# Spreading a head's projections between its tiles, sharing the mask's pieces among three engines, and all transfers of p on one queue, in a graph attention kernel with layer norm

## Chip, cores and metric

One Trainium2 chip, one core. The metric is the device time of the kernel in microseconds (us), the median of several executions; a profile is one execution. PE (TensorE) multiplies, DVE (VectorE), ACT (ScalarE) and POOL (GpSimd) work on elements, SP (SyncE) only issues transfers (DMAs); ACT can issue them too.

## What is computed

```python
def reference(x, adj, Wq, Wk, Wv, Wout):          # x (2048, 256), adj (2048, 2048), W (256, 2048)
    q = (x @ Wq).reshape(8, 2048, 256)            # a head is 256 rows of x @ W, read as 2048 x 256
    k = (x @ Wk).reshape(8, 2048, 256)
    v = (x @ Wv).reshape(8, 2048, 256)
    a = q @ k.T / 16 + adj + adj                  # per head
    a = where(adj == 0, -1e6, a); a = softmax(a); a = where(adj == 0, 0, a)
    out = (a @ v).transpose(1, 0, 2).reshape(2048, 2048) @ Wout
    return layernorm(x + out)                     # over the last axis, eps 1e-5
```

Nearly all of adj is zero (about 1 element in 256 is not).

## The kernel before

Every factor of a product is split into a high part and a low part (`k_split`, `q_split`, `v_split`, `p_split`, `w_slot`), the high by an ACT copy, the low by a subtraction on DVE or POOL, and a product is the sum of three partial products. There are 8 heads, and in each 16 tiles of 128 query rows (`tau` counts tiles over all heads, 0 to 127; h is the head and t the tile in it).

A tile goes through these steps. PE makes the scores of 128 rows against 2048 columns in four banks (`scores`, L367). DVE adds the mask M (adj, and minus a huge number where adj is zero) and takes maxima (`score`, L591), then the row's maximum (L603). ACT takes exp over the whole row (`exp_tile`, L497). DVE transposes p in blocks of 32 (`turn`, L611), DMAs move the blocks to their places in `p_turned` (`shuffle`: for each quarter i of the row four transfers j, two issued by SP at L257 and two by ACT at L516). ACT writes the high part of each quarter (`hi_p`, L506), POOL the low part (`lo_p`, L449). PE multiplies by v three tiles later (`values(tau - LAG)`, L386 to L390), with Wout already in v, and DVE divides by the row's sum and adds to y (`add_y`, L633, L636).

A head needs 33 projections: k0 to k7, q0 to q7, vt0 to vt7 (x times Wv, transposed), v0 to v7 (vt times Wout) and the transpose of its rows of x. Each takes a bank, a copy on ACT (L491) and a subtraction on DVE (L579, L575). The k and q0 come in one row ahead of tile 0, the vt and v in one row ahead of tile 3, and q1 to q7 within the even tiles. The weights come through five slots (loaded at L226, high part L483, low part L438). Scores and projections take the six banks in turn, in the order in which `in_order` names them.

In head 0 the mask is built too, one tile ahead. `build(t, q)` takes a piece of adj (128x512, loaded at L242 into one of two places in the unused part of `y_acc`), marks its zeros (L645) and writes the mask's piece (L650), both on DVE. `store_m` saves each tile's mask in memory, and ACT loads it again for heads 1 to 7. At the end 15 tiles are normalised (L696) after the last y is complete, then the last one.

Each engine runs its list in order. Waits on semaphores alone tie the lists together, and an engine or a queue that waits holds all that stands behind it.

## Time and profile before

| | |
|---|---|
| median of 3 runs | 2012.87 us (2012.28 to 2017.43) |
| the profiled execution's own time | 2015.95 us |
| its span, first to last instruction | 2014.2 us |
| busy: PE, DVE, ACT, POOL | 92%, 57%, 41%, 45% of the span |
| PE busy in the first fifth and later | 4 to 8 tenths, then 9 or more |
| mean granted clock of PE | 0.96 of 2.4 GHz |
| transfers of p | 2048 of 64 KB, half each on SP and ACT, 2.0 and 2.1 us from issue to landing |

A busy share says how long an engine had an instruction in work, not that it set the pace. A wait row says which engine stood idle, and what came last before it went on. Times within the span count from its first instruction.

### The profile page before, as it was taken

Reading aid. Unit: us, or ns where it says so; the run is one execution under the profiler, and the core shown is the slowest. Engines: PE = TensorE matmul, PEld = TensorE weight load, DVE = VectorE, ACT = ScalarE, POOL = GpSimd, SP = SyncE. Lnnn points to the kernel's source line nnn. Section 1 sums busy time; section 2 is a strip of 40 time slices with the busy share of each in tenths; the row PEclk is TensorE's granted clock in tenths of the full one; section 3 lists DMA queues with packets and bytes.
Section 4 is the critical chain, followed back from the end, with each engine's and each line's share of the span. In section 5 each row is a group of like instructions: output and inputs, shape, how many; then the busy total and the mean of one; then the engine's idle time right before and its main releaser. Section 6 shows DMA issues by size and latency. Waiting matters only on the chain.

```text
span 2014.2 us, 29280 instructions
## 1 busy us (share of the span) xinstructions
PE 1854.8 (92%) x10272; PEld 1611.9 (80%) x10272; DVE 1152.2 (57%) x2356; ACT 819.3 (41%) x1364; POOL 904.8 (45%) x718
## 2 busy tenths in 40 slices
PE   6487768799999999999999999899999999999996
PEld 5376657698888888898887988798888988888885
DVE  6567877455555555545564555555554555655664
ACT  3232212443454443444444533453444443544432
POOL 4133222545454454544445454554454454544442
PEclk9698888899999999999999999999999999999998
DMA  5645555646665566556665466555665466654663
GB/s 171 186 129 175 170 177 184 182 135 190 193 192 167 149 181 193 173 150 178 197 202 148 149 186 191 173 158 166 189 194 165 145 184 189 202 165 136 182 177 95
DMA packets 186931, 345.97 MB, mean 172 GB/s; under 512 B 39328, under 2 KB 96672, under 8 KB 170400
## 3 DMA queue, kind: packets, MB, share of 16 engines
q10 hardware_dynamic: 65280, 184.62, 29.8%
q1 hardware_dynamic: 121504, 159.47, 28.5%
q8 instruction: 82, 1.34, 0.3%
q14 instruction: 65, 0.53, 0.1%
HBM read 190.84 MB, written 18.87 MB: 104 GB/s over the span
## 4 chain that ended last, share of the span: by engine, by line
PE 75%; POOL 2%; issue 2%; DMA 2%; DVE 1%; ACT 1%; SPq 0%; ACTq 0%; POOLq 0%; DVEq 0%
PE bank L367 31%; PE y_bank L390 19%; PE bank L339 13%; PE y_bank L388 10%; PE y_bank L386 1%; POOL w_slot L438 1%; DMA raw_w<-in_L_gnn_Wk_dram 1%; POOL p_split L449 1%; DVE y_acc L696 0%; DVE vt_split L579 0%; DMA m_dram<-m_sb 0%; SPq L257 0%; ACT t_p L497 0%; ACT w_slot L483 0%; DMA y_acc<-in_adj_dram 0%
## 5 line engine op out<-in xcount | busy, mean ns | idle before, releaser
L449 POOL TENSOR_TENSOR p_split<-p_turned,p_split 128x512 fp32r<-128x512 f32 x512 | 649.2, 1297 | 844.2 <-ACT p_split L506 843.0
L367 PE MATMUL bank<-k_split,q_split 128*128 128x512 f32 x3072 | 800.0, 396 | 27.5 <-issue 16.7
L390 PE MATMUL y_bank<-v_split,p_split 128*128 128x512 f32 x1920 | 710.6, 403 | 0.0
L367 PEld LDWEIGHTS bank<-k_split,q_split 128*128 128x128 f32 x3072 | 584.9, 191 | 142.4 <-issue 18.2
L497 ACT ACTIVATE t_p<-t_p,small 128x2048 f32<-128x2048 f32 x128 | 257.1, 2009 | 871.8 <-DVE small L603 866.6
L591 DVE CUSTOM_DVE_ANT_0 t_p<-bank,m_sb 128x512 f32<-128x512 f32 x512 | 351.0, 687 | 427.2 <-PE bank L367 408.4
L388 PE MATMUL y_bank<-v_split,p_split 128*128 128x256 f32 x2048 | 561.3, 285 | 0.0
L390 PEld LDWEIGHTS y_bank<-v_split,p_split 128*128 128x128 f32 x1920 | 367.3, 191 | 79.6
L388 PEld LDWEIGHTS y_bank<-v_split,p_split 128*128 128x128 f32 x2048 | 395.3, 193 | 23.3
L438 POOL TENSOR_TENSOR w_slot<-raw_w,w_slot 128x512 fp32r<-128x512 f32 x192 | 249.2, 1306 | 243.9 <-ACT w_slot L483 240.9
L339 PE MATMUL bank<-x_t,w_slot 128*128 128x256 f32 x2304 | 312.0, 290 | 39.1 <-POOL w_slot L438 28.3
L339 PEld LDWEIGHTS bank<-x_t,w_slot 128*128 128x128 f32 x2304 | 301.1, 198 | 49.6 <-POOL w_slot L438 29.8
L611 DVE STREAM_TRANSPOSE blocks<-t_p 128x2048 f32<-128x2048 f32 x128 | 295.6, 2309 | 75.0 <-ACT t_p L497 70.0
L506 ACT ACTIVATE p_split<-p_turned 128x512 fp32r<-128x512 f32 x512 | 283.5, 617 | 10.5 <-issue 5.6
L483 ACT ACTIVATE w_slot<-raw_w 128x512 fp32r<-128x512 f32 x192 | 118.4, 624 | 65.4 <-DMA raw_w<-in_L_gnn_Wv_dram 26.0
L339 PE MATMUL bank<-w_out,vt_split 128*128 128x256 f32 x768 | 105.5, 288 | 23.2 <-DVE vt_split L579 23.2
L339 PEld LDWEIGHTS bank<-w_out,vt_split 128*128 128x128 f32 x768 | 97.8, 194 | 26.6 <-DVE vt_split L579 26.6
L633 DVE SCALAR_TENSOR_TENSOR y_acc<-y_bank,small,y_acc 128x256 f32<-128x256 f32 x128 | 61.9, 484 | 63.6 <-PE y_bank L390 63.2
L386 PE MATMUL y_bank<-v_split,p_split 128*128 128x512 f32 x128 | 54.7, 428 | 44.4 <-POOL p_split L449 44.4
L645 DVE TENSOR_SCALAR_CACHE_REDUCE zero_mark<-y_acc 128x512 uint8<-128x512 f32 x64 | 43.8, 684 | 68.0 <-DMA y_acc<-in_adj_dram 67.7
L579 DVE TENSOR_TENSOR k_split<-bank,k_split 128x512 fp32r<-128x512 f32 x64 | 43.5, 686 | 64.0 <-ACT k_split L491 64.0
L650 DVE SCALAR_TENSOR_TENSOR m_sb<-zero_mark,y_acc 128x512 f32<-128x512 uint8 x64 | 77.5, 1211 | 3.3
(43 smaller groups left out, 630.1 us busy)
## 6 DMA issues: line engine op xcount, KB each, us to landing
m_sb<-m_dram ACTq DMA_DIRECT2D x112, 1024.0 KB, 4.9
p_turned<-blocks SPq DMA_DIRECT2D x1024, 64.0 KB, 2.0
p_turned<-blocks ACTq DMA_DIRECT2D x1024, 64.0 KB, 2.1
raw_w<-in_L_gnn_Wk_dram SPq DMA_DIRECT2D x64, 256.0 KB, 3.8
y_acc<-in_adj_dram SPq DMA_DIRECT2D x64, 256.0 KB, 3.2
raw_w<-in_L_gnn_Wq_dram SPq DMA_DIRECT2D x64, 256.0 KB, 3.2
m_dram<-m_sb SPq DMA_DIRECT2D x16, 1024.0 KB, 3.9
raw_w<-in_L_gnn_Wv_dram SPq DMA_DIRECT2D x64, 256.0 KB, 3.4
```

The lines of the kernel that those rows point to most:

```text
L339: mm = nc.tensor.matmul(dst[:, o * R:(o + 1) * R], left[:, a, k, o * P:(o + 1) * P], right[:, b, k, :], start=(i == 0), stop=(i == len(TER ...
L367: mm = nc.tensor.matmul(dst[:], q[:, a, k, f * P:(f + 1) * P], k_split[:, kk, k, b * BANK:(b + 1) * BANK], start=(i == 0), stop=(i == len( ...
L388: nc.tensor.matmul(y[:, 0:D], lo, v_split[:, j, HI], start=False, stop=False)
L390: mm = nc.tensor.matmul(y[:], hi, v_split[:, j].rearrange("p s d -> p (s d)"), start=False, stop=last)
L438: nc.gpsimd.tensor_tensor(w[:, LO], raw_slot[n % SLOTS][:], w[:, HI].bitcast(F32), ALU.subtract).then_inc(w_lo, 1)
L449: nc.gpsimd.tensor_tensor(lo, p_turned[:, i * BANK:(i + 1) * BANK].rearrange("p (j b) -> p j b", b=QUAD), hi.bitcast(F32), ALU.subtract).t ...
L483: nc.scalar.activation(w[:, HI], raw_slot[n % SLOTS][:], ACT.Copy).then_inc(w_hi, 1)
L497: nc.scalar.activation(t_p[:], t_p[:], ACT.Exp, bias=neg_max[:, t:t + 1], scale=1.0, accum_out=row_sum[:, t:t + 1]).then_inc(exp_done, 1)
L506: nc.scalar.activation(by_chunk(p_split[tau % 2][:, HI])[:, :, i, :], p_turned[:, i * BANK:(i + 1) * BANK].rearrange("p (j b) -> p j b", b ...
L591: nc.vector.tensor_tensor_reduce(out=t_p[:, b * BANK:(b + 1) * BANK], in0=bank[r][:], in1=m_sb[tau % 2][:, b * BANK:(b + 1) * BANK], scale ...
L611: nc.vector.transpose(blocks[tau % 2][:].rearrange("p (q j b) -> p j q b", q=QUADS, b=QUAD), t_p[:].rearrange("p (j q b) -> p j q b", q=QU ...
L650: nc.vector.scalar_tensor_tensor(out=m_sb[t % 2][:].rearrange("p (c r) -> p c r", c=C)[:, :, q * rows:(q + 1) * rows], in0=zero_mark[:].re ...
```

## The change

1. **Projections between the tiles.** `due(tau, b)` lists what stands behind bank b of tile tau, on every engine. In head 0 only k0, k1 and q0 come before tile 0; k2 to k7 stand between its banks, vt and v in tiles 0 to 2. In later heads k0 to k6 stand in tile 15 of the head before, k7 in tile 0, vt and v in tiles 1 to 3.
2. **The mask.** Of the four pieces of a tile the odd ones are built as before. The even ones are marked by DVE, scaled by ACT (`scale_mark`) into the mask, and adj is added by POOL (`add_adj`).
3. **Adjacency a tile ahead.** The loads for tile t + 2 stand behind the transfers of tile t − 1. There are four places up to piece 43, the last of tile 10, and two from then on.
4. **Transfers.** All 16 of a tile are issued by SP, none by ACT.
5. **Norm in parts.** Tiles 0 to 11 are normalised after y of tile 12 (iteration 128), 12 to 14 after y of tile 14, and the last at the end.

```diff
-        Y_LATE = TILES - 4
-        adj_chunk = [y_acc[:, Y_LATE + 2 * i:Y_LATE + 2 * i + 2, :].rearrange("p a d -> p (a d)") for i in range(2)]
-        zero_mark = sbuf("zero_mark", [P, BANK], U8)
+        Y_MID, Y_LATE = TILES - 8, TILES - 4
+        adj_place = [y_acc[:, Y_MID + 2 * i:Y_MID + 2 * i + 2, :].rearrange("p a d -> p (a d)") for i in range(4)]
+        FOUR_PLACES = 11 * BANKS
+        adj_at, adj_nth, adj_uses = [], [], [0] * 4
+        for a in range(TILES * BANKS):
+            place = a % 4 if a < FOUR_PLACES else 2 + a % 2
+            adj_uses[place] += 1
+            adj_at.append(place)
+            adj_nth.append(adj_uses[place])
...
+        FIRST_V = {(0, 3): (("vt", 0), ("vt", 1)), (1, 0): (("v", 0), ("vt", 2)), (1, 1): (("v", 1), ("vt", 3)),
...
+        NEXT_K = {(TILES - 1, 0): (0,), (TILES - 1, 1): (1, 2), (TILES - 1, 2): (3, 4), (TILES - 1, 3): (5, 6)}
+        def due(tau, b):
+            h, t = divmod(tau, TILES)
+            if h >= H:
+                return
+            for c in FIRST_K.get((t, b), ()) if h == 0 else ((C - 1,) if (t, b) == (0, 0) else ()):
+                yield "k", h, c
+            if t % 2 == 0 and t <= LAST_Q and b == (3 if tau == 0 else 1):
+                yield "q", h, t // 2 + 1
+            for kind, c in (LATER_V if h else FIRST_V).get((t, b), ()):
+                yield kind, h, c
+            if h + 1 < H:
+                if (t, b) == (TURN_X, 1):
+                    yield "x", h + 1
+                if (t, b) == (TILES - 2, 2):
+                    yield "q", h + 1, 0
+                for c in NEXT_K.get((t, b), ()):
+                    yield "k", h + 1, c
...
-            if t == 0:
-                for c in range(C):
-                    in_order(("k", h, c))
-                in_order(("q", h, 0))
-            if t == VALUES_FROM:
-                for c in range(C + 1):
-                    if c < C:
-                        in_order(("vt", h, c))
-                    if c:
-                        in_order(("v", h, c - 1))
             for b in range(BANKS):
                 in_order(("s", tau, b))
-                if b == 1 and t % 2 == 0 and t <= LAST_Q:
-                    in_order(("q", h, t // 2 + 1))
-                if b == 1 and t == TURN_X and h + 1 < H:
-                    in_order(("x", h + 1))
+                for key in due(tau, b):
+                    in_order(key)
...
+        EARLY_NORM = TILES - 4
+        NORM_PARTS = [slice(0, EARLY_NORM), slice(EARLY_NORM, TILES - 1), slice(TILES - 1, TILES)]
...
+        def m_piece(a):
+            t, q = divmod(a, BANKS)
+            rows = BANK // C
+            return m_sb[t % 2][:].rearrange("p (c r) -> p c r", c=C)[:, :, q * rows:(q + 1) * rows]
...
                     t, q = divmod(a, BANKS)
-                    if a >= 2:
-                        sp.wait_ge(m_chunk, a - 1)
-                    sp.dma_start(adj_chunk[a % 2], adj_rows[t // 2, t % 2][:, q * BANK:(q + 1) * BANK]
-                                 ).then_inc(adj_loaded[a % 2], 16)
+                    place = adj_at[a]
+                    if adj_nth[a] > 1:
+                        m_of(max(b for b in range(a) if adj_at[b] == place))
+                    sp.dma_start(adj_place[place], adj_rows[t // 2, t % 2][:, q * BANK:(q + 1) * BANK]
+                                 ).then_inc(adj_loaded[place], 16)
...
-                    for j in range(QUADS // 2):
+                    for j in range(QUADS):
...
+                load_w(SLOTS + len(START))
                 for tau in range(ALL + 1):
                     h, t = divmod(tau, TILES)
                     if h == 0:
+                        if t == 0:
+                            for i in range(BANKS):
+                                load_adj(BANKS + i)
+                            load_wout(0)
                         store_m(t)
-                        if t == 1:
-                            for f in range(HALVES):
-                                sp.dma_start(y_tokens[:, f, :Y_LATE // 2], x_tokens[f][:, :Y_LATE // 2]
-                                             ).then_inc(y_init, 16)
+                        if t == 2:
+                            load_y(0, Y_MID // 2, y_init)
+                        if t == 10:
+                            load_y(Y_MID // 2, Y_LATE // 2, y_mid)
...
+                        if tau < ALL:
+                            load_w(w_by[tau, i] + SLOTS)
                         if tau:
                             shuffle(tau - 1, i)
-                        if h == 0 and t + 1 < TILES:
-                            load_adj((t + 1) * BANKS + i)
-                    if opens:
-                        load_w_behind("q", h, 0)
-                    if sums:
-                        load_w_behind("vt", h, C - 1)
-                    if tau < ALL and t % 2 == 0 and t <= LAST_Q:
-                        load_w_behind("q", h, t // 2 + 1)
+                        if h == 0:
+                            load_adj((t + 2) * BANKS + i)
...
                 def project_x(key):
+                    wait_emptied(("x", key[1]))
                     pe.wait_ge(w_lo, w_order[key] + 1)
                     project(key, w_of(key), x_t)
+                def project_v(key):
+                    kind, h, c = key
+                    pe.wait_ge(wout_lo, h + 1)
+                    wait_emptied(("vt", h, c))
+                    project(key, vt_split[c % 2], w_out)
...
+                        for key in due(tau, g):
+                            if key[0] == "x":
+                                turn_x(key[1])
+                            elif key[0] == "v":
+                                project_v(key)
+                            else:
+                                project_x(key)
...
+                def add_adj(a):
+                    t, q = divmod(a, BANKS)
+                    m = m_piece(a)
+                    pool.wait_ge(m_scaled, a // 2 + 1)
+                    nc.gpsimd.tensor_tensor(m, m, adj_place[adj_at[a]].rearrange("p (r c) -> p c r", c=C),
+                                            ALU.add).then_inc(m_by_pool, 1)
...
+                    for b in range(BANKS):
+                        if 2 <= tau < ALL + 2:
+                            lo_p(tau - 2, b)
+                        if tau + 1 < TILES and b in (1, 3):
+                            add_adj((t + 1) * BANKS + b - 1)
+                        for key in due(tau, b):
+                            if key in w_order:
+                                lo_w(w_order[key] + 3)
...
-                def shuffle(tau, i):
-                    if i == 0:
-                        act.wait_ge(turned, tau + 1)
-                    if tau:
-                        act.wait_ge(p_lo, 4 * (tau - 1) + i + 1)
-                    for j in range(QUADS // 2, QUADS):
-                        act.dma_start(p_turned[quad(j), i * BANK:(i + 1) * BANK],
-                                      blocks[tau % 2][quad(i), j * BANK:(j + 1) * BANK]).then_inc(shuffled[i], 16)
...
+                def scale_mark(a):
+                    t, q = divmod(a, BANKS)
+                    if t >= 2:
+                        act.wait_ge(m_stored, 16 * (t - 1))
+                        act.wait_ge(max_ready, t - 1)
+                    act.wait_ge(marked, a + 1)
+                    nc.scalar.activation(m_piece(a), zero_mark[0][:].rearrange("p (r c) -> p c r", c=C), ACT.Copy,
+                                         scale=-BIG).then_inc(m_scaled, 1)
...
+                    dve.wait_ge(adj_loaded[adj_at[a]], 16 * adj_nth[a])
+                    if q % 2 == 0 and a:
+                        dve.wait_ge(m_scaled, a // 2)
+                    if q % 2 and a > 1:
+                        dve.wait_ge(m_by_dve, a // 2)
+                    nc.vector.tensor_scalar(mark[:], adj_piece, 0.0, None, ALU.is_equal, ALU.add,
                                             accum_out=chunk_count[:, q:q + 1]).then_inc(marked, 1)
-                    if q == 0 and t >= 2:
-                        dve.wait_ge(m_stored, 16 * (t - 1))
-                    dve.wait_ge(marked, a + 1)
-                    nc.vector.scalar_tensor_tensor(
-                        out=m_sb[t % 2][:].rearrange("p (c r) -> p c r", c=C)[:, :, q * rows:(q + 1) * rows],
-                        in0=zero_mark[:].rearrange("p (r c) -> p c r", c=C), scalar=-BIG,
-                        in1=adj_chunk[a % 2].rearrange("p (r c) -> p c r", c=C),
-                        op0=ALU.mult, op1=ALU.add).then_inc(m_chunk, 1)
+                    if q % 2:
+                        if t >= 2:
+                            dve.wait_ge(m_stored, 16 * (t - 1))
+                        dve.wait_ge(marked, a + 1)
+                        nc.vector.scalar_tensor_tensor(
+                            out=m_piece(a), in0=mark[:].rearrange("p (r c) -> p c r", c=C), scalar=-BIG,
+                            in1=adj_piece.rearrange("p (r c) -> p c r", c=C),
+                            op0=ALU.mult, op1=ALU.add).then_inc(m_by_dve, 1)
...
+                            if tau + 1 < TILES:
                                 build(t + 1, b)
+                        for key in due(tau, b):
+                            lo_of(key)
                     if tau == ALL:
                         denominator(tau - 1)
-                all_vars(0, slice(0, TILES - 1))
-                all_vars(1, slice(TILES - 1, TILES))
-                inverse_std(0, slice(0, TILES - 1))
-                normalise(0, TILES - 1)
-                inverse_std(1, slice(TILES - 1, TILES))
-                normalise(TILES - 1, TILES)
+                        all_vars(0, NORM_PARTS[0])
+                        inverse_std(0, NORM_PARTS[0])
+                        normalise(NORM_PARTS[0])
+                    if tau == ALL + LAG - 1:
+                        all_vars(1, NORM_PARTS[1])
+                        inverse_std(1, NORM_PARTS[1])
+                        normalise(NORM_PARTS[1])
+                all_vars(2, NORM_PARTS[2])
+                inverse_std(2, NORM_PARTS[2])
+                normalise(NORM_PARTS[2])```

On DVE, in a tile of head 0 from the turn on, before: `score` is the row of two ISA instructions, and each L645 (mark) is followed by its L650 (mask piece); `m_chunk` counts pieces.

```order
L611 STREAM_TRANSPOSE blocks<-t_p 128x16x4x32 [waits shuffled3,shuffled2,exp_done,shuffled1,shuffled0]
L591 ISA t_p,small<-bank,m_sb 128x512 [waits m_chunk,turned,scores_done]
L591 ISA small 128x1
L618 SCALAR_TENSOR_TENSOR small<-small 128x1 [waits floor_done]
L622 RECIPROCAL small<-small 128x1 [waits denom_ready]
L645 TENSOR_SCALAR zero_mark,small<-y_acc 128x512 [waits m_chunk,adj_loaded0]
L650 SCALAR_TENSOR_TENSOR m_sb<-zero_mark,y_acc 128x8x64 [waits marked,m_stored]
L591 ISA t_p,small<-bank,m_sb 128x512 [waits m_chunk,scores_done]
```

The same place after the change.

```order
L626 STREAM_TRANSPOSE blocks<-t_p 128x16x4x32 [waits shuffled3,shuffled2,exp_done,shuffled1,shuffled0]
L606 ISA t_p,small<-bank,m_sb 128x512 [waits m_by_pool,m_by_dve,turned,scores_done]
L606 ISA small 128x1
L633 SCALAR_TENSOR_TENSOR small<-small 128x1 [waits floor_done]
L637 RECIPROCAL small<-small 128x1 [waits denom_ready]
L664 TENSOR_SCALAR zero_mark,small<-y_acc 128x512 [waits m_scaled,adj_loaded0]
L606 ISA t_p,small<-bank,m_sb 128x512 [waits scores_done]
L606 ISA small 128x1
L664 TENSOR_SCALAR zero_mark,small<-y_acc 128x512 [waits m_by_dve,adj_loaded1]
L670 SCALAR_TENSOR_TENSOR m_sb<-zero_mark,y_acc 128x8x64 [waits marked,m_stored]
```

Piece 0 has lost its mask instruction on DVE, piece 1 keeps it, and the tile's first score now waits for the mask of POOL (`m_by_pool`).

On SP, at the start of a tile of head 0, before: the store of the mask, two transfers of p for a quarter, then the load of a piece of adj.

```order
L249 DMA m_dram<-m_sb 128x2048 [waits m_stored,m_chunk]
L257 DMA p_turned<-blocks 32x512 [waits p_lo,turned]
L257 DMA p_turned<-blocks 32x512
L242 DMA y_acc<-in_adj_dram 128x512 [waits m_chunk]
L257 DMA p_turned<-blocks 32x512 [waits p_lo]
```

The same place after the change.

```order
L289 DMA m_dram<-m_sb 128x2048 [waits m_stored,m_by_dve,m_by_pool]
L302 DMA p_turned<-blocks 32x512 [waits p_lo,turned]
L302 DMA p_turned<-blocks 32x512 x3
L281 DMA y_acc<-in_adj_dram 128x512 [waits m_by_pool]
L302 DMA p_turned<-blocks 32x512 [waits p_lo]
```

Four transfers stand where two stood, and the load between the quarters waits for a mask piece of the next tile, half of the time one of POOL's.

On PE, between the last banks of head 0 and the row of k of head 1, before (L339 is a projection, L388 and L390 are values).

```order
L388 MATMUL y_bank<-v_split,p_split 128x256
L390 MATMUL y_bank<-v_split,p_split 128x512
L339 MATMUL bank<-x_t,w_slot 128x256 [waits emptied2,w_lo,emptied3]
L339 MATMUL bank<-x_t,w_slot 128x256 x11
L339 MATMUL bank<-x_t,w_slot 128x256 [waits emptied3,w_lo]
L339 MATMUL bank<-x_t,w_slot 128x256 x11
L339 MATMUL bank<-x_t,w_slot 128x256 [waits emptied4,w_lo]
```

The same after the change, in tile 15 of head 0.

```order
L401 MATMUL bank<-k_split,q_split 128x512 [waits emptied1]
L401 MATMUL bank<-k_split,q_split 128x512 x5
L366 MATMUL bank<-x_t,w_slot 128x256 [waits emptied2,w_lo,emptied3]
L366 MATMUL bank<-x_t,w_slot 128x256 x11
L366 MATMUL bank<-x_t,w_slot 128x256 [waits emptied3,w_lo]
L366 MATMUL bank<-x_t,w_slot 128x256 x11
L422 MATMUL y_bank<-v_split,p_split 128x256
L424 MATMUL y_bank<-v_split,p_split 128x512
```

Nine projections in a row have become one or two between scores and values; elsewhere `due` sets up to five (behind bank 1 of tile 2).

## Rows read from the trace of the kernel before

**Rows 1.** Busy time by stretch, of windows in us.

```profile
core 0: us, PE busy (x) PEld busy (x) DVE busy (x) ACT busy (x) POOL busy (x), PEclk, DMA share, GB/s
150.00:345.00 195.00, 146.27 (x669) 120.82 (x669) 148.50 (x308) 50.54 (x82) 54.61 (x44) 0.86 0.55 172
410.00:1980.00 1570.00, 1542.15 (x8703) 1345.47 (x8702) 868.26 (x1776) 688.00 (x1144) 753.98 (x595) 0.99 0.60 174
```

**Rows 2.** The turns in five stretches: count, ns min/median/max, first and last start.

```profile
L611 DVE STREAM_TRANSPOSE blocks<-t_p x4: 2300/2302/2311, 46.7 to 135.5; 128x2048 f32<-128x2048 f32 x4
...
L611 DVE STREAM_TRANSPOSE blocks<-t_p x12: 2300/2302/2311, 135.5 to 344.5; 128x2048 f32<-128x2048 f32 x12
...
L611 DVE STREAM_TRANSPOSE blocks<-t_p x3: 2300/2302/2312, 344.5 to 389.4; 128x2048 f32<-128x2048 f32 x3
...
L611 DVE STREAM_TRANSPOSE blocks<-t_p x97: 2300/2311/2315, 389.4 to 1780.8; 128x2048 f32<-128x2048 f32 x97
...
L611 DVE STREAM_TRANSPOSE blocks<-t_p x16: 2303/2311/2314, 1780.8 to 1980.2; 128x2048 f32<-128x2048 f32 x16
```

**Rows 3.** Waits from 150 to 345 us: total, times, longest in us.

```profile
PE y_bank L386 <- POOL p_split L449: 42.0, 9, 6.2
DVE zero_mark L645 <- DMA y_acc<-in_adj_dram: 38.7, 15, 4.2
```

**Rows 4.** Timeline of one tile of head 0: start, us, engine, idle before.

```profile
270.63 1.15 SPq L257 DMA_DIRECT2D p_turned<-blocks  x2
...
271.83 0.58 SPq L242 DMA_DIRECT2D y_acc<-in_adj_dram  x1
...
275.49 0.69 DVE L645 TENSOR_SCALAR_CACHE_REDUCE zero_mark<-y_acc 128x512 uint8<-128x512 f32 x1 [3.51 <-DMA y_acc<-in_adj_dram]
```

**Rows 5.** Issues of p's transfers on SP, and the page's time to landing.

```profile
499.62 3.12 SPq L257 DMA_DIRECT2D p_turned<-blocks  x5
...
L257 SPq DMA_DIRECT2D p_turned<-blocks x1024: 507/591/2089, 49.0 to 1986.9; - x171
...
p_turned<-blocks SPq DMA_DIRECT2D x1024, 64.0 KB, 2.0
```

**Rows 6.** L650 as a line, and one of it beside a GpSimd instruction.

```profile
L650 DVE SCALAR_TENSOR_TENSOR m_sb<-zero_mark,y_acc x64: 1083/1180/2183, 12.4 to 341.9; 128x512 f32<-128x512 uint8 x64
...
102.13 1.26 POOL L449 TENSOR_TENSOR p_split<-p_turned,p_split 128x512 fp32r<-128x512 f32 x1
...
102.15 2.18 DVE L650 SCALAR_TENSOR_TENSOR m_sb<-zero_mark,y_acc 128x512 f32<-128x512 uint8 x1
```

**Rows 7.** PE at the row of k of head 2, and the window behind it.

```profile
595.26 3.14 PE L339 MATMUL bank<-x_t,w_slot 128*128 128x256 f32 x24 [0.76 <-POOL w_slot L438]
599.01 3.14 PE L339 MATMUL bank<-x_t,w_slot 128*128 128x256 f32 x24 [0.61 <-POOL w_slot L438]
604.43 2.02 PE L367 MATMUL bank<-k_split,q_split 128*128 128x512 f32 x5 [2.28 <-issue]
...
604.00:609.00 5.00, 4.57 (x15) 3.86 (x16) 1.42 (x5) 1.15 (x2) 3.63 (x3) 0.66 0.39 108
```

**Rows 8.** The last low part of a tile, and the values that read it.

```profile
499.90 1.28 POOL L449 TENSOR_TENSOR p_split<-p_turned,p_split 128x512 fp32r<-128x512 f32 x1
...
507.36 0.39 PE L386 MATMUL y_bank<-v_split,p_split 128*128 128x512 f32 x1
```

**Rows 9.** Timeline of the end.

```profile
1969.03 2.31 DVE L611 STREAM_TRANSPOSE blocks<-t_p 128x2048 f32<-128x2048 f32 x1
...
1990.09 1.28 ACT L521 ACT_TABLE_LOAD   x1
...
1993.65 0.50 PE L386 MATMUL y_bank<-v_split,p_split 128*128 128x512 f32 x1 [0.35 <-POOL p_split L449]
...
1999.16 0.39 PE L390 MATMUL y_bank<-v_split,p_split 128*128 128x512 f32 x1
...
2002.80 4.93 DVE L696 TENSOR_SCALAR y_acc<-y_acc,ln 128x256 f32<-128x256 f32 x15
...
2008.61 0.41 DVE L696 TENSOR_SCALAR y_acc<-y_acc,ln 128x256 f32<-128x256 f32 x1
```

More of the change, by code:

```diff
@@ L249, in store_m, with load_y @@
                     sp.dma_start(m_dram[t], m_sb[t % 2][:]).then_inc(m_stored, 16)
+                def load_y(c_first, c_stop, loaded_sem):
+                    for f in range(HALVES):
+                        sp.dma_start(y_tokens[:, f, c_first:c_stop], x_tokens[f][:, c_first:c_stop]
+                                     ).then_inc(loaded_sem, 16)
                 def shuffle(tau, i):
@@ L306, in _ @@
+                    if t == 5 and h + 1 < H:
+                        load_wout(h + 1)
                     if t == LAST_Q and h + 1 < H:
@@ L628, in add_y @@
                         dve.wait_ge(y_init, 32)
+                    if tau == Y_MID:
+                        dve.wait_ge(y_mid, 32)
                     if tau == Y_LATE:
@@ L692, in inverse_std, with normalise @@
                     dve.wait_ge(ln_step, 5 * part + 5)
-                def normalise(first, stop):
-                    for t in range(first, stop):
+                def normalise(tiles):
+                    for t in range(tiles.start, tiles.stop):
                         nc.vector.tensor_scalar(y_acc[:, t, :], y_acc[:, t, :], mean_var[:, t, 0:1], inv[:, t:t + 1],
@@ L705, in _ @@
                             moments((tau - LAG - 1) % TILES)
[L706 to L728 removed]
+                    if 1 <= tau <= ALL:
                         turn(tau - 1)
```

218 lines of the change are left out of this document (73 added, 145 removed).

## The prediction

> **What bounds the kernel now.** I read the busy time by stretches first, since the page's digits for TensorE (PE) are low only in the first fifth. Between 410 and 1980 us PE works 1542.2 of 1570 us; between 150 and 345 us, in head 0, only 146.3 of 195 us, at a granted clock of 0.86, while VectorE (DVE) works 148.5 us [rows 1]. Then the turns of the tiles (L611, one per tile), whose first and last starts give each stretch's pace [rows 2]: tiles 3 to 14 of head 0 take 209.0 us for 11, 19.0 each; turn 16 starts at 389.4; from there six heads take 1391.4 us, 231.9 each, 14.5 a tile.
>
> So there are two kernels in one. From head 1 on PE sets the pace and the rest fits beneath it. In head 0 the waits [rows 3] name another bound: DVE waits 38.7 us for the adjacency in 195 us, 3.9 a tile, and PE 42.0 us for the low parts of p. The timeline of one tile [rows 4] shows why the first is late: SP issues the load at 271.83, behind two transfers of p that themselves waited for the turn, and DVE can use it at 275.49. The other 15.1 us of the pitch are DVE's own instructions, and PE waits for a chain that DVE starts.
>
> **The change, part by part.**
>
> *Adjacency a tile ahead.* It removes the 3.9 us wait as long as there are four places, so for the pieces that are built up to tile 10. 19.0 − 3.9 = 15.1.
>
> *Half of the mask pieces to ScalarE and GpSimd.* Two of four L650 a tile leave DVE: 1.18 us each in the median [rows 6], 2.3 with their overlap: 15.1 − 2.3 = 12.8 us. GpSimd gets two additions a tile. The trace has none of that form; its nearest row is 1.26 us (a subtraction of the same 128x512), and its upper bound takes the ratio of DVE's strided 1.18 to a contiguous 0.69 [rows 4, 6], so 1.3 to 2.2; I take 1.3, as the subtraction of p is also written in blocks. ScalarE gets two copies at 0.62 to 1.1. Both have room in head 0. But DVE meets GpSimd: an L650 at 102.15 took 2.18 us, 1.0 more, beside a GpSimd subtraction that began 0.02 us before it [rows 6]. In head 0 the changed GpSimd works some 10 of 13 us (four subtractions of p, two additions, 1.5 of weights, all at 1.3), so I charge the remaining two L650 0.6 each: 12.8 + 1.2 = 14.0. Bounds 12.8 (never) and 14.8 (both by 1.0).
> The Trainium skill (SBUF — State Buffer, Who interferes with whom) says that a VectorE instruction with two SBUF inputs and a GpSimd instruction that reads SBUF exclude each other, the later waiting in full. Row 102.15 agrees; by that rule the change puts more of such work on GpSimd just when DVE's rest must pass it, and 14.0 rather than 12.8 follows from it too.
>
> The change adds a wait to the tile's first score: POOL's addition to piece 2 must be done, or DVE and with it the next exp stand. Counted from the tile's first score, DVE marks piece 2 at about 6.6 us, ScalarE copies by 7.3, GpSimd, which has by then finished the low parts of p (from 2.0 us before the first score, 4 x 1.3 with one addition between), adds by 8.6. The next first score comes at 14.0, so 5 us cover it. ScalarE's copy stands ahead of exp, whose row maximum is ready at 7.8: nothing on the path either, as long as p's last quarter has landed by then.
>
> *Sixteen transfers on the sync queue.* SP issues p's pieces 0.62 us apart (3.12 us for five), and its adjacency loads cost about 0.58 [rows 4, 5]. A tile of head 0 then needs 16 x 0.62 + 4 x 0.6 + 0.3 (store) + 0.6 (about one weight) = 13.2 us of issuing, just under 14.0. Moreover the queue now waits in the middle: the load for tile t+2 stands between pieces of p of tile t−1, and waits for a build of tile t+1. With four places that build is early. From tile 11 on there are two, so pieces 2 and 3 wait for pieces 0 and 1 of their own tile to be built, as now. I walk this chain by hand: score and mark 2.0 us, copy 0.7, addition 1.3, load issued 0.6 and landed 3.1 later (271.83 to 275.49 is 3.7 [rows 4]), against a mark that wants it at 6.6 us; about 1 to 3 us of waiting come back. The pieces of p behind that load land near 10 us into the next tile; ScalarE takes them before its exp, so exp and turn slip as well. I put these five tiles (10 to 14) at 17.5 us; bounds 14.0 and 19.0.
> From head 1 on, 16 x 0.62 + 1.5 x 0.6 = 10.8 us of issuing fit into 14.5, and into the shortest tile, 11.1 (turns at 1969.0 and 1980.2 [rows 2, 9]). The last piece lands 2.5 (turn) + 9.9 + 2.0 = 14.4 us after exp instead of some 9.5, but ScalarE reads it only behind the next exp, 11.1 + 2.2 later, and the low part follows 1.3 later: PE needed it some 6 us after it was ready (a low part ends at 501.2, its values start at 507.4 [rows 8]). The weights' loads ahead of p's quarters wait for the projection of the same bank: one q in an even tile is done about 4 us after exp, before the second quarter's turn at 5.0; where several projections stand behind a bank (tiles 1, 2, 3 and 15) a quarter waits some 6 us more. I cost all of this at nothing; its cover is LAG, three tiles, and if that were gone the price is 1 to 4 us a tile.
> The Trainium skill (DMA: Bandwidth & Descriptors, Issuing engines are not separate DMA queues) says that several issuing engines save only the sequencer's time. By that, ScalarE's share, 8 x 0.62 = 5.0 us a tile, is simply moved to SP: no bandwidth is lost, and none gained.
>
> *Projections spread.* From head 1 on they take PE the same time. What goes is the waiting around the row of k: 0.76 + 0.61 + 2.28 us at 595 to 604, and the half clock after it (0.66 granted over 604 to 609, 1.7 us) [rows 7]. With two keys between scores, each weight is split some 4 us before use. 231.9 − 5.4 = 226.5 a head; six heads: −32. Bounds: 0 and −36.
> In head 0, turns 0 to 3 take 88.8 us now [rows 2], with the block of v in it. Then tile 0 is a chain of k, split, scores three times over, so turn 0 starts at 49 instead of 46.7. Tiles 1 and 2 get 15 keys at 0.7 us of DVE each: 11.8 (14.0, less 1.0 for y, less 1.2, as GpSimd is freer there) + 5.4 = 17 each; tile 3 is 15. Turn 3: 98 instead of 135.5, −37. Bounds ±10.
> The end of head 0, turns 14 to 16, takes 44.9 us, of which DVE waits for k a good part. With seven keys spread over tile 15, PE needs 11.1 + 7 x 1.45 = 21.2 and 12.6 for the next: 33 to 34. −11.
>
> *Norm in parts.* Now 14.6 us pass between PE's last product (1999.6) and the end: 15 tiles are normalised at 0.33 (4.93), then the last at 2008.61, stored by 2014.2 [rows 9]. With one tile left behind it: 1.1 for y, 0.65 moments, 1.6 for the root and its steps, 0.4, and about 3.9 for one store (two take 5.2 now) = 7.6; −7. But the first part stands on DVE before y of tile 125, and waits for a root on ScalarE that stands behind the splits of p of tile 127. Those come late: the turn ends at 1982.5, sixteen issues take 9.9, landing 2.0 [rows 5], split 0.6, table load 1.28, steps 1.2, twelve tiles 4.0, y 1.0: PE may start the last values at 2002.5 instead of 1993.65, and after such a gap at half clock: +9 to +11. Net +3; bounds −7 and +5.
>
> **Sum.** Turn 3 at 98; six tiles (4 to 9) at 14.0: 182; five at 17.5: 269.5; two: 303. Now 389.4, so −86. Heads −32, tail +3: 2014.2 − 115 = 1899 for the span, and 1.8 around it (its own time is 2015.95): 1901. The median of the runs, 2012.9, lies 3 below that execution's own time: **1898 us**.
> Its own range: the six tiles 12.8 to 14.8 (−7, +5), the five −17 to +8, opening ±10, heads −4 to +32, tail −10 to +2. These hardly fall together; 1875 to 1925.
>
> **Rivals.**
> *A, DVE alone paces head 0* (20%): the queue's waits stay hidden, eleven tiles at 13.0 instead of 171.5 in all: −28, tail −5: 1865. For it: 13.2 of issuing is below 14, and a landed piece has slack before its exp. Against: the two-place stretch has a wait inside one tile.
> *B, the sync queue paces more than that* (20%): loads keyed to builds hold back p everywhere in head 0 and at projections in later heads, where a weight's load waits for PE and p waits behind it. Eleven tiles at 18.5: +32; or 1 us a tile in the burst tiles of seven heads: +15 to +20. About 1940. For it: the adjacency wait of today is the same kind, a load behind p in one queue. Against: LAG.
> *C, slower than before* (4%): issuing alone bounds every tile. Heads 1 to 7 have 17.5 issues a tile; at 0.62 they need 10.8. To lose the 115 us they must exceed 14.2 + 115/112 = 15.2, so 0.87 us an issue. At 1.0 each: 17.5 x 112 = 1960 instead of 1590, so about 2270. For it: single issues reach 2.09 us [rows 5]. Against: the median is 0.59 while the other queue issues too.
> *D, the adjacency wait stays* (4%), since a load a tile ahead still stands behind p: 11 x 3.0: 1930.
> The forecast itself: 52%.
>
> Faster or slower by 0.3% (6 us, about what a measurement of this kernel can tell from no change): faster 95%, same 1%, slower 4%. The range goes from 10 below A, its half of the opening's spread, up to B: 1855 to 1940.
>
> **What would show it.** Right: pitch of L611 near 14 in tiles 4 to 9, 17 in 10 to 14, 226.5 a head after; no PE wait at k; DVE waits for the adjacency only from tile 10; L670 (now L650) near 1.8 in the mean; values of the last tile starting near 2002 − 115. Wrong: a pitch below 13 in tiles 10 to 14 (the hand walk is too pessimistic), idle PE in heads 1 to 7 with p's low part as its releaser (SP's issuing shows through), or turn 3 later than 115.

## The result and the profile after

The changed kernel takes 1946.85 us in the median of 4 runs (1943.55 to 1949.04), against 2015.15 (2012.28 to 2018.61) for the kernel before, run beside it: a ratio of 0.9659, 95% interval 0.9635 to 0.9683. It is faster, and 49 us slower than forecast, outside the range. Its profiled execution spans 1941.8 us, where the prediction's terms, unrounded, give 302.5 to turn 16 + 1359 for six heads + 236.4 for the rest = 1897.9. That is 43.9 us to find.

The turns of the tiles, of the kernel after (count, ns min/median/max, first and last start), in the stretches of [rows 2]; the turn is now L626:

```profile
L626 DVE STREAM_TRANSPOSE blocks<-t_p x3: 2302/2311/2311, 45.5 to 81.7; 128x2048 f32<-128x2048 f32 x3
L626 DVE STREAM_TRANSPOSE blocks<-t_p x6: 2299/2300/2302, 95.6 to 168.0; 128x2048 f32<-128x2048 f32 x6
L626 DVE STREAM_TRANSPOSE blocks<-t_p x3: 2300/2301/2302, 182.1 to 219.5; 128x2048 f32<-128x2048 f32 x3
L626 DVE STREAM_TRANSPOSE blocks<-t_p x4: 2300/2302/2314, 237.0 to 311.6; 128x2048 f32<-128x2048 f32 x4
L626 DVE STREAM_TRANSPOSE blocks<-t_p x96: 2311/2311/2315, 325.6 to 1693.3; 128x2048 f32<-128x2048 f32 x96
L626 DVE STREAM_TRANSPOSE blocks<-t_p x16: 2311/2311/2312, 1707.3 to 1906.0; 128x2048 f32<-128x2048 f32 x16
```

| stretch | predicted us | measured us | difference |
|---|---|---|---|
| start to turn 3 | 98 | 95.6 | −2.4 |
| turns 3 to 9 | 84 | 86.5 | +2.5 |
| turns 9 to 14, of which 12 to 13 | 87.5, 17.5 | 96.9, 25.2 | +9.4, +7.7 |
| turns 14 to 16 | 33 | 46.7 (32.6 and 14.0) | +13.7 |
| six heads | 1359 (226.5 each) | 1381.7 (230.3 each) | +22.7 |
| turn 112 to the end | 236.4 | 234.5 | −1.9 |

So the opening, the pitch under four places and that under two (17.3, 20.0 and 17.5 for the first three) came near what I had worked out. Two stretches of head 0 (turns 12 to 13 and 14 to 15) and one in each later head did not. The waits of the kernel after (total, times, longest in us) name that of the heads:

```profile
DVE y_acc L650 <- PE y_bank L424: 51.7, 114, 3.3
...
PE bank L386 <- DMA raw_x<-in_x_dram: 38.5, 8, 12.6
...
PE y_bank L420 <- POOL p_split L472: 30.4, 12, 7.3
...
PE bank L366 <- issue: 15.3, 2, 13.9
...
DVE zero_mark L664 <- DMA y_acc<-in_adj_dram: 12.4, 9, 4.0
```

The adjacency wait is down to 12.4 us. Before, it was 67.7 over the whole run, with the 38.7 of [rows 3] in it. None of the 12.4 comes before 192.3 us, at a piece of tile 11, the first under two places, as forecast. In its place stands a wait of 38.5 us that I never costed: PE, about to transpose the next head's rows of x (`turn_x`, L386), waits for their load. The kernel before had 10.5 us of it in two waits, one at the start and one in head 0, and none in the later heads. The timeline of SP in head 1 (start, duration in us) shows why:

```profile
485.52 5.66 SPq L302 DMA_DIRECT2D p_turned<-blocks  x9
491.22 0.58 SPq L249 DMA_DIRECT2D raw_x<-in_x_dram  x1
493.19 11.71 SPq L302 DMA_DIRECT2D p_turned<-blocks  x16
```

PE at the same time, and the windows behind it (the granted clock is the third number from the right):

```profile
496.33 1.09 PE L386 MATMUL bank<-ident,raw_x 128*128 128x128 f32 x4 [3.22 <-DMA raw_x<-in_x_dram]
...
496.00:501.00 5.00, 4.67 (x15) 4.08 (x16) 0.69 (x1) 1.63 (x3) 2.35 (x2) 0.50 0.29 70
501.00:506.00 5.00, 5.00 (x24) 4.13 (x23) 1.34 (x4) 0.00 (x0) 0.16 (x1) 0.86 0.43 105
```

`load_x` is the last entry of SP's iteration 12 of a head, in which it issues the transfers of tile 11. Its place in the list has not moved, but ahead of it now stand sixteen transfers of p instead of eight. It is issued at 491.22 and lands at 496.20; PE reaches its transpose after 3.2 us of idling, and runs the next stretch at half its clock (0.50 granted, the lower of its two levels). Heads 1 to 6 wait 2.9 to 4.5 us at this place, 22.1 in all, head 0 12.6. (The first wait of the eight, 3.8 us, is that of the start, as before.) In head 0 adjacency loads stand in the same queue too, and SP stands still for 2.3 us at one of them, between 241.1 and 243.5 us, before it comes to x at 246.93.

The other loss is on ACT in head 0; timeline of the kernel after, ACT and SP, then PE:

```profile
274.12 2.00 ACT L524 ACTIVATE t_p<-t_p,small 128x2048 f32<-128x2048 f32 x1
...
289.73 0.34 ACTq L544 DMA_DIRECT2D m_sb<-m_dram  x1
290.18 0.63 ACT L533 ACTIVATE p_split<-p_turned 128x512 fp32r<-128x512 f32 x1 [13.79 <-DMA m_dram<-m_sb]
...
279.56 4.95 SPq L302 DMA_DIRECT2D p_turned<-blocks  x8
284.62 0.52 SPq L289 DMA_DIRECT2D m_dram<-m_sb  x1
...
293.48 2.90 PE L366 MATMUL bank<-x_t,w_slot 128*128 128x256 f32 x12 [13.93 <-issue]
```

ACT reloads the first mask from memory (`load_m(16)`, L544) once the last one is stored. Its wait stands ahead of all copies of its iteration; the store is issued by SP only at 284.62, again behind a tile's transfers of p. ACT stands 13.79 us, the banks with projections of k are not emptied, and PE stands 13.93. The profile calls PE's wait "issue": it names no releaser, and only the order in time leads to ACT.

### The profile page after: what moved, and what is told of

Same layout as the page of the kernel before. It is cut to its first block, busy times and chain, and to the rows that moved or that the text cites. A ratio compares the mean times of both kernels' runs of the same rounds, so it can differ in the third digit from the quotient of the medians.

```text
span 1941.8 us, 29208 instructions
## 1 busy us (share of the span) xinstructions
PE 1830.8 (94%) x10272; PEld 1596.6 (82%) x10272; DVE 1134.8 (58%) x2330; ACT 851.9 (44%) x1397; POOL 974.8 (50%) x750
## 3 DMA queue, kind: packets, MB, share of 16 engines
q8 instruction: 82, 1.34, 0.3%
## 4 chain that ended last, share of the span: by engine, by line
PE 76%; SPq 4%; DMA 2%; issue 2%; DVE 1%; POOL 1%; ACT 0%; DVEq 0%; ACTq 0%
PE bank L401 29%; PE y_bank L424 19%; PE bank L366 16%; PE y_bank L422 10%; SPq L302 4%; DMA raw_x<-in_x_dram 1%; PE y_bank L420 1%; DVE blocks L626 1%; DMA p_turned<-blocks 0%; POOL p_split L472 0%; PE bank L386 0%; DVE y_acc L715 0%; ACT t_p L524 0%; POOL w_slot L461 0%; SPq L261 0%
## 5 line engine op out<-in xcount | busy, mean ns | idle before, releaser
L472 POOL TENSOR_TENSOR p_split<-p_turned,p_split 128x512 fp32r<-128x512 f32 x512 | 661.1, 1308 | 619.6 <-ACT p_split L533 619.4
L401 PE MATMUL bank<-k_split,q_split 128*128 128x512 f32 x3072 | 794.0, 394 | 6.9 <-DVE k_split L593 4.7
L424 PE MATMUL y_bank<-v_split,p_split 128*128 128x512 f32 x1920 | 713.0, 404 | 0.0
L401 PEld LDWEIGHTS bank<-k_split,q_split 128*128 128x128 f32 x3072 | 581.3, 190 | 119.0 <-issue 5.3
L606 DVE CUSTOM_DVE_ANT_0 t_p<-bank,m_sb 128x512 f32<-128x512 f32 x512 | 351.8, 687 | 404.9 <-PE bank L401 383.5
L422 PE MATMUL y_bank<-v_split,p_split 128*128 128x256 f32 x2048 | 562.2, 285 | 0.0
L424 PEld LDWEIGHTS y_bank<-v_split,p_split 128*128 128x128 f32 x1920 | 368.7, 192 | 78.1
L524 ACT ACTIVATE t_p<-t_p,small 128x2048 f32<-128x2048 f32 x128 | 256.8, 2006 | 357.7 <-DVE small L618 357.7
L422 PEld LDWEIGHTS y_bank<-v_split,p_split 128*128 128x128 f32 x2048 | 395.8, 193 | 18.7
L461 POOL TENSOR_TENSOR w_slot<-raw_w,w_slot 128x512 fp32r<-128x512 f32 x192 | 255.0, 1329 | 299.0 <-ACT w_slot L510 296.2
L533 ACT ACTIVATE p_split<-p_turned 128x512 fp32r<-128x512 f32 x512 | 303.7, 622 | 199.7 <-DMA p_turned<-blocks 185.3
L626 DVE STREAM_TRANSPOSE blocks<-t_p 128x2048 f32<-128x2048 f32 x128 | 295.8, 2311 | 81.6 <-ACT t_p L524 79.7
L366 PE MATMUL bank<-x_t,w_slot 128*128 128x256 f32 x2304 | 305.7, 284 | 18.0 <-issue 15.3
L366 PEld LDWEIGHTS bank<-x_t,w_slot 128*128 128x128 f32 x2304 | 298.0, 193 | 28.1 <-issue 18.9
L518 ACT ACTIVATE q_split<-bank 128x512 fp32r<-128x512 f32 x64 | 38.3, 598 | 161.0 <-PE bank L366 161.0
L366 PEld LDWEIGHTS bank<-w_out,vt_split 128*128 128x128 f32 x768 | 98.7, 191 | 6.1 <-POOL w_out L466 2.8
L366 PE MATMUL bank<-w_out,vt_split 128*128 128x256 f32 x768 | 101.2, 283 | 2.4 <-POOL w_out L466 2.4
L650 DVE SCALAR_TENSOR_TENSOR y_acc<-y_bank,small,y_acc 128x256 f32<-128x256 f32 x128 | 61.9, 483 | 51.7 <-PE y_bank L424 51.7
L420 PE MATMUL y_bank<-v_split,p_split 128*128 128x512 f32 x128 | 52.7, 412 | 39.3 <-POOL p_split L472 30.4
L518 ACT ACTIVATE v_split<-bank 128x512 fp32r<-128x512 f32 x64 | 38.2, 597 | 92.7 <-PE bank L366 92.7
```

What stands on the lines that cost most here:

```text
L366: mm = nc.tensor.matmul(dst[:, o * R:(o + 1) * R], left[:, a, k, o * P:(o + 1) * P], right[:, b, k, :], start=(i == 0), stop=(i == len(TER ...
L401: mm = nc.tensor.matmul(dst[:], q[:, a, k, f * P:(f + 1) * P], k_split[:, kk, k, b * BANK:(b + 1) * BANK], start=(i == 0), stop=(i == len( ...
L422: nc.tensor.matmul(y[:, 0:D], lo, v_split[:, j, HI], start=False, stop=False)
L424: mm = nc.tensor.matmul(y[:], hi, v_split[:, j].rearrange("p s d -> p (s d)"), start=False, stop=last)
L461: nc.gpsimd.tensor_tensor(w[:, LO], raw_slot[n % SLOTS][:], w[:, HI].bitcast(F32), ALU.subtract).then_inc(w_lo, 1)
L472: nc.gpsimd.tensor_tensor(lo, p_turned[:, i * BANK:(i + 1) * BANK].rearrange("p (j b) -> p j b", b=QUAD), hi.bitcast(F32), ALU.subtract).t ...
```

## The experiments

Each is the changed kernel with one edit, in the last two with several, timed in three rounds against the kernel before.

### The load of x ahead of the transfers

```diff
@@ SP, for each quarter i
                             load_w(w_by[tau, i] + SLOTS)
+                        if i == 1 and t == LAST_Q and h + 1 < H:
+                            load_x(h + 1)
                         if tau:
                             shuffle(tau - 1, i)
...
-                    if t == LAST_Q and h + 1 < H:
-                        load_x(h + 1)
```

> Only the load of the next head's rows of x moves: in tile 12 it stands before the transfers of p's second quarter instead of behind all sixteen, about 12 issues (8 us) earlier. Theory (the load's place in the sync queue makes PE wait): the wait at the transpose of x, 38.5 us in eight places, falls below 12 us, a head from 230.3 to about 226.5 us, tile 13 of head 0 from 25.2 to about 17.5; span 1941.8 - 30 = about 1912. Rival (the queue as a whole is late, and x with it): the wait moves to p's low part or to the weights, and the span stays above 1935.

Measured: 1903.62 us (1902.32 to 1905.32), ratio 0.9447 (0.9426 to 0.9468), 43 us below the changed kernel. From head 1 on no wait for x is left, and the six heads take 224.6 each, 1.9 less than I had forecast (turns of this run):

```profile
L626 DVE STREAM_TRANSPOSE blocks<-t_p x96: 2310/2311/2315, 319.6 to 1653.2; 128x2048 f32<-128x2048 f32 x96
L626 DVE STREAM_TRANSPOSE blocks<-t_p x16: 2311/2311/2312, 1667.2 to 1865.8; 128x2048 f32<-128x2048 f32 x16
...
PE bank L386 <- DMA raw_x<-in_x_dram: 6.5, 2, 3.9
```

The windows over the same six heads, from turn 16 to turn 112, of the kernel before, of the changed one, and of this one (PE's busy time is the first number after the comma):

```profile
389.40:1780.80 1391.40, 1363.87 (x7706) 1190.37 (x7705) 760.34 (x1543) 612.19 (x1022) 676.51 (x534) 0.99 0.60 175
```

```profile
325.60:1707.30 1381.70, 1359.57 (x7705) 1189.84 (x7705) 757.07 (x1542) 620.21 (x1021) 681.76 (x534) 0.99 0.62 176
```

```profile
319.60:1667.20 1347.60, 1347.60 (x7706) 1182.10 (x7705) 756.52 (x1542) 622.89 (x1022) 681.29 (x534) 1.00 0.63 181
```

PE is busy for all of 1347.6 us here, at the full clock: these matmuls, in this order, leave no idle time to remove. The changed kernel's 34.1 us above it are 22.1 of waiting and 12.0 of the same matmuls taking longer at the lower clock; 3.7 and 2.0 a head. In head 0 turns 12 to 13 fall from 25.2 to 17.8 us, near the forecast's pitch of 17.5, and turn 16 comes 6.0 earlier.

### The first reload of the mask behind the copies

```diff
@@ ACT, iteration tau
-                    if TILES <= tau + 1 < ALL:
+                    if TILES < tau + 1 < ALL:
                         load_m(tau + 1)
                     for b in range(BANKS):
...
+                    if tau + 1 == TILES:
+                        load_m(TILES)
```

> Only ScalarE's load of the mask of tile 16 moves behind the rest of its work in iteration 15, so that its wait for the last store of the mask holds nothing up. Theory (this wait of 13.8 us holds k's high parts and with them PE, 13.9 us at 293.5): turns 14 to 16 take about 34 to 38 us instead of 46.7, span about 1930. Rival (the load itself is late, or the store stands behind the transfers of p on SP, and the first score of head 1 waits for the mask just as long): DVE waits for the mask instead, span above 1938.

Measured: 1941.99 us (1939.62 to 1945.17), ratio 0.9642 (0.9616 to 0.9668). ACT's 13.8 us are gone, PE has two waits of 2.3 left, and turns 14 to 16 take 38.6 instead of 46.7 us: 8.1 saved there, a little less than the 8.7 to 12.7 that I expected. The span, 1937.9, missed its 1930. The median gained 4.9. In the profiled execution the wait for x in head 0 was 14.1 instead of 12.6 us, and turn 16 came 6.2 earlier. DVE waits 0.4 us for the mask, not as long as the rival had it. So ACT's wait is what held PE, as far as 8.1 us; in the median the intervals of the two kernels overlap.

### The first part of the norm an iteration later

```diff
@@ DVE, behind y of an iteration
                         denominator(tau - 1)
+                    if tau == ALL + LAG - 2:
                         all_vars(0, NORM_PARTS[0])
```

> Only the first part of the norm moves behind y of tile 125. Theory (it held that y, and PE's last values, for 8.9 us): the last values start about 6 us earlier, when p's low part is ready at 1921.7, and the span falls by 4 to 6, to about 1937. Rival (the late transfers of p alone set the end): no change within 1 us, 1941.

Measured: 1943.69 us (1938.56 to 1945.12), ratio 0.9641 (0.9616 to 0.9665). The changed kernel first, then this one (timelines of DVE and PE at the end):

```profile
1921.91 0.23 DVE L698 RECIPROCAL ln<-ln 128x12 f32<-128x12 f32 x1 [11.48 <-ACT ln L539]
1922.99 3.96 DVE L715 TENSOR_SCALAR y_acc<-y_acc,ln 128x256 f32<-128x256 f32 x12
1928.02 0.77 PE L420 MATMUL y_bank<-v_split,p_split 128*128 128x512 f32 x1 [8.90 <-DVE y_acc L653]
```

```profile
1928.32 0.50 PE L420 MATMUL y_bank<-v_split,p_split 128*128 128x512 f32 x1 [2.73 <-POOL p_split L472]
1929.57 3.96 DVE L715 TENSOR_SCALAR y_acc<-y_acc,ln 128x256 f32<-128x256 f32 x12
```

The last values no longer wait for the norm, only 2.73 us for p. From turn 112 to the end it takes 229.6 us (1713.8 to 1943.4) instead of 234.5: 4.9 us of the norm's cost were the wait that it puts ahead of y. The median does not resolve it: 3.2 us less, with overlapping intervals. In this execution turn 16 came 2.7 us later than in the changed kernel's, and the six heads took 3.9 more.

### Half of the transfers back on ScalarE

```diff
@@ SP, shuffle
-                    for j in range(QUADS):
+                    for j in range(QUADS // 2):
@@ ACT, as in the kernel before
+                def shuffle(tau, i):
...
+                    for j in range(QUADS // 2, QUADS):
```

> Half of p's transfers go back to ScalarE, 8 on each queue; all else as in the changed kernel. Theory (what was lost against the forecast is the sync queue's lateness for x and the last mask store, 10 us of issuing a tile instead of 5): x's wait in later heads falls below 1 us, heads at 226 to 227, tiles 10 to 13 of head 0 shorter, end 5 us earlier: span 1895 to 1915. Rival (ScalarE's queue, which now waits for projections in between, delays its half of p more than SP did): idle PE for p's low part, span 1935 or more.

Measured: 1911.48 us (1910.43 to 1915.70), ratio 0.9490 (0.9467 to 0.9513). Four of the six heads take 224.6 to 225.1 us, one 225.9, and one 231.4, in which PE waits 5.1 us for x. So the move of all transfers to SP is what makes the load of x late in the later heads. In head 0 taking half of them back does not help: the longest of this run's waits for x (total, times, longest) still stands there:

```profile
PE bank L386 <- DMA raw_x<-in_x_dram: 23.7, 4, 14.7
```

Here x stands behind eight transfers instead of sixteen, and behind the same adjacency loads: SP stands still for over 4 us at two of them (239.2 to 243.5 and 247.4 to 251.5 us). Turn 16 comes at 328.0, no earlier than in the changed kernel: turns 3 to 9 take 91.8 us against 86.5, a loss whose cause was not taken apart, and turns 14 to 16 take 41.6 against 46.7. The end takes 229.8 against 234.5. Moving the load alone (1903.6) undoes the damage better than moving the transfers back.

### All mask pieces on VectorE

```diff
@@ DVE, build
-                    if q % 2:
+                    if True:
@@ ACT, and add_adj on POOL likewise
-                            scale_mark((t + 1) * BANKS + b - 1)
```

> The changed kernel with all four mask pieces of a tile built by VectorE, none by ScalarE and GpSimd. Theory 1 (contention takes back half): the two pieces that stay on VectorE cost 2.08 us in the changed kernel against 1.18 before, since GpSimd adds beside them. With four pieces and no additions on GpSimd the piece falls to 1.2 to 1.5 us, so VectorE pays 4 x 1.3 = 5.2 us a tile instead of 4.2; tiles 4 to 9 come every 15.0 us instead of 14.1, and the whole is 5 to 15 us slower than the changed kernel (1952 to 1962). Theory 2 (the sharing was worth what was taken off VectorE): two pieces of 1.18 come back in full beside two that stay at 2.1; pitch 16.5, 25 us or more slower. Theory 3 (the transfers' queue sets the pace anyway): pitch 14.1, no change.

Measured: 1952.85 us (1948.33 to 1956.11), ratio 0.9683 (0.9658 to 0.9707); 6 us slower than the changed kernel, with overlapping intervals. The traces, below, show more than the medians. The mask piece as a line, of the changed kernel (L670), then of this one (L666):

```profile
L670 DVE SCALAR_TENSOR_TENSOR m_sb<-zero_mark,y_acc x32: 1183/2082/2690, 12.4 to 275.7; 128x512 f32<-128x512 uint8 x32
```

```profile
L666 DVE SCALAR_TENSOR_TENSOR m_sb<-zero_mark,y_acc x64: 1086/1182/2262, 7.7 to 283.7; 128x512 f32<-128x512 uint8 x64
```

Twice 2.08 in the median is 4.2 us a tile, four times 1.18 is 4.7: the sharing saved half a microsecond a tile on this instruction, not the 2.3 that left VectorE. Turn 3 comes 8.7 us later here (104.3). Turns 3 to 9 take 91.4 us (15.2 a tile) and 86.5 in the changed kernel (14.4): the sharing is worth 0.8 a tile. Turns 9 to 12 are quicker without it (15.6, 16.5 and 17.0 against 17.3, 20.0 and 17.5, 5.7 us in all), and VectorE's wait for the adjacency falls from 12.4 to 2.1 us. The likely reason, not tested by itself: with two places a load waits for a piece of its own tile, and a piece that passes through three engines is ready later.

### Two places from tile 4

```diff
-        FOUR_PLACES = 11 * BANKS
+        FOUR_PLACES = 4 * BANKS
```

> The changed kernel with four places for the adjacency only up to tile 3 and two from tile 4, where the changed kernel has four up to tile 10. Theory 1 (the two places make the pitch of tiles 10 to 12, 17.3, 20.0 and 17.5 us, since a load then waits for a build of its own tile): tiles 3 to 9 rise from some 14.3 to 17.5 to 19 each, the adjacency wait of VectorE from 12.4 to over 30 us in all, and the time by 20 to 30 us (about 1970 to 1975). Theory 2 (those tiles are slow for something else, such as the projections of x or the queue's issuing): tiles 4 to 9 stay near 14.1 and the time within 5 us of the changed kernel.

Measured: 1971.32 us (1968.21 to 1973.16), ratio 0.9780 (0.9763 to 0.9797), 24.5 us slower than the changed kernel. Its turns 3 to 9 and its wait for the adjacency:

```profile
L626 DVE STREAM_TRANSPOSE blocks<-t_p x7: 2299/2302/2304, 100.8 to 205.2; 128x2048 f32<-128x2048 f32 x7
...
DVE zero_mark L664 <- DMA y_acc<-in_adj_dram: 35.8, 26, 3.8
```

Turns 3 to 9 take 104.4 us, 17.4 a tile instead of 14.4. That is the 17.5 of the hand walk, and the adjacency wait rises from 12.4 to 35.8. The four places, and not the queue position alone, carry the gain of the "tile ahead".

### The three moves together, and with half the transfers on ScalarE

The edits of the first three experiments in one kernel:

> The changed kernel with three moves together: the load of the next head's x ahead of the transfers of tile 13, the first reload of the mask behind them on ScalarE, and the first part of the norm one iteration later. If the three stalls are separate, the gains add to that of the load of x alone (1903.6): less 8 for turns 14 to 16 and 5 for the tail, 1887 to 1895, and the interval of turn 14 near 24.5 and the last values' wait near 2.7 us as in the single runs. If head 0 is bound by the transfers behind the stall, what is saved at the mask's reload comes back as another wait in tiles 14 to 16, and the time stays near 1898 to 1900.

Measured: 1894.72 us (1891.94 to 1895.90), ratio 0.9399 (0.9384 to 0.9415). 8.9 below the load of x alone; the profiled span is 7.9 below. Here its turns 3 to 8, and those of its heads:

```profile
L628 DVE STREAM_TRANSPOSE blocks<-t_p x6: 2301/2302/2303, 98.2 to 170.7; 128x2048 f32<-128x2048 f32 x6
...
L628 DVE STREAM_TRANSPOSE blocks<-t_p x96: 2311/2311/2316, 316.9 to 1650.4; 128x2048 f32<-128x2048 f32 x96
L628 DVE STREAM_TRANSPOSE blocks<-t_p x16: 2311/2311/2314, 1664.4 to 1863.0; 128x2048 f32<-128x2048 f32 x16
```

The tail takes 229.5 us (5.1 less than with the load alone), but head 0 gained only 2.7. Turns 14 to 16 take 40.1 us, 6.4 less than with the load alone; but turn 3 comes 1.5 later, and turns 12 to 13 went from 17.8 to 21.3, with a wait for x of 3.6 instead of 2.6 us and 0.71 of the clock granted from 245 to 250 us behind it, instead of 1.00. These losses lie ahead of the mask's reload, so they are not its price; why they came was not taken apart.

The same, with ScalarE issuing half of the transfers:

> The same three moves, and half of p's transfers issued by ScalarE as before the change. If issuing on the sync queue still holds something back once the three stalls are gone, this beats the three moves alone by 3 us or more; if it mattered only through the load of x (the single run with half on ScalarE gave 1911.5), there is nothing left to gain, and ScalarE's eight issues a tile delay its copies in head 0: 1890 to 1900, the same as the three moves or up to 8 us slower.

Measured: 1893.95 us (1891.74 to 1894.99), ratio 0.9396 (0.9381 to 0.9411): the same in the median. Its turns 3 to 8, and the last 16:

```profile
L641 DVE STREAM_TRANSPOSE blocks<-t_p x6: 2311/2311/2314, 100.8 to 178.8; 128x2048 f32<-128x2048 f32 x6
...
L641 DVE STREAM_TRANSPOSE blocks<-t_p x16: 2311/2311/2316, 1666.2 to 1863.0; 128x2048 f32<-128x2048 f32 x16
```

The same time hides differences that cancel. With half on ScalarE, turn 3 comes 2.6 us later, turns 3 to 9 take 92.5 us against 86.5, turns 9 to 14 89.1 against 92.1, turns 14 to 16 34.7 against 40.1, the six heads 1.6 more in all, and the end 225.4 against 229.5. So neither way is better for the whole kernel: sharing the issues costs in the first half of head 0 and pays in the second, and at the end of the kernel. Why was not taken apart.

## Why the prediction was off

**The step that failed** is under "Sixteen transfers on the sync queue": "I cost all of this at nothing; its cover is LAG, three tiles". I weighed p's own pieces and the weights behind the transfers. The load of x and the store of the last mask also stand in that queue, and LAG covers neither: x is wanted by PE within the next tile, the store by ACT at once. Restoring x's lead alone gave 43 us. That it is nearly the whole miss in the median (49) is partly chance, for the items are not the same: in the traces it is 34.1 in the heads (the 22.7 missed and 11.4 more, by which they came out below my 226.5 each) and 6 in head 0. In head 0 taking half of the transfers off SP did not make x earlier (the wait was 14.7 us); the adjacency loads ahead of it, which wait for builds, stand in that queue too. I had counted that wait for p alone.

**Turns 14 to 16.** "PE needs 21.2 and 12.6 for the next" counted PE's work. The time was ACT's wait for the mask's store, 8.1 us by its experiment. The rest of the 13.7, some 5.6, was not isolated, but about as much goes with the transfers: with half of them back on ScalarE the stretch fell from 46.7 to 41.6, and in the kernel of three moves from 40.1 to 34.7, within 2 us of the forecast.

**Rival B** had nearly the right time (1940) and half the mechanism: the sync queue does hold back PE in every head. But it let weights and p be late. No wait for either is among PE's in heads 1 to 6, and the single item is the transpose of x. It was priced at 1 us a tile in the burst tiles; what came was 5.7 us once a head. The time was luck: its own terms, +32 or +15 to +20 on 1898, give 1930 or at most 1918, and not 1940.

**Adjacency and its places** held: 14.4 against 14.0 a tile under four places, 17.3 to 20.0 against 17.5 under two, and undoing the places cost 24.5 us.

**The mask pieces** held in the sum and not in the reasons. The base was right: with four pieces on VectorE and the wait gone a tile took 15.2 us, forecast 15.1. (I called all 15.1 VectorE's own work; in the kernel before it was 14.4, 158.2 us of busy time for the 11 tiles from 135.5 to 344.5 us.) The sharing gained 0.8 instead of 1.1. I charged the two pieces that stay 0.6 each for GpSimd; they cost 0.9 more each in the median of the whole run (1.98 us in the mean, where I had put 1.8). In turns 3 to 9 the pieces took 4.4 us a tile of VectorE, against 4.8 with all four on it: 0.4 of the 0.8, and the rest was not isolated. One case of the changed kernel's timeline, DVE and then POOL:

```profile
158.37 2.24 DVE L670 SCALAR_TENSOR_TENSOR m_sb<-zero_mark,y_acc 128x512 f32<-128x512 uint8 x1
...
157.91 1.65 POOL L479 TENSOR_TENSOR m_sb<-m_sb,y_acc 128x512 f32<-128x512 f32 x1 [1.71 <-ACT m_sb L552]
```

At 158.37 the addition had 1.19 us to go; 1.19 + 1.18 is 2.37, near the 2.24 taken. By the rule of the Trainium skill (SBUF — State Buffer, Who interferes with whom) that a VectorE instruction with two SBUF inputs and a GpSimd instruction that reads SBUF exclude each other, the trace agrees. It is more than an incidental meeting here: the sharing itself puts GpSimd's addition of one piece just ahead of VectorE's next piece, so that 29 of the 32 pieces meet one. GpSimd's addition took 1.66 in the median (1.3 was taken); DVE's scores never waited for it.

**Heads.** The saving at the row of k was 5.4 by [rows 7]; with x restored it is 231.9 − 224.6 = 7.3. The windows of six heads show the 1.9 that I missed: the kernel before waited 27.5 us (4.6 a head, where the three rows of one head gave 3.65), and its matmuls took 16.3 more (2.7 a head, where one window gave 1.7).

**Norm in parts** cost +3 by my sum, +1.1 in the trace (234.5 against 233.4), by the wait that I named: the last values start 220.7 us after turn 112 (1928.02 − 1707.3), forecast 221.7 (2002.5 − 1780.8). Without that wait it would have been a gain of 3.8 (229.6).

## What to carry to other kernels

When transfers are moved onto a queue, list everything that stands behind them there, and for each item who wants it and how soon; the rare ones (a load once a head, one last store) cost more than the frequent ones that have slack. Place a load by when it is wanted, ahead of the bulk, rather than at the end of an iteration. Before giving VectorE's two-input work to GpSimd, count what stays on VectorE at its price beside GpSimd: here 2.3 us a tile taken off bought 0.8, and nothing but a loss where the longer way of a piece held up the next load.

## What the runs showed of the hardware that I had not expected

- A short wait costs PE more than its length: waits of 3.7 us in the mean were worth 5.7 a head, with 0.50 and 0.86 of the clock granted in the two 5 us windows behind one.
- With all 16 transfers of a tile issued by SP, landing took 2.4 us in the median, 2.0 and 2.1 before; the masks' reloads landed in 5.9, 4.9 before. The total does not show it: with half the transfers on ScalarE (2.0 and 2.3 us, reloads 5.1) the best version took the same time.
